# Moving one of ten chunks a tile from VectorE to ScalarE, dropping the first layer's split, and reordering the products behind the loop

## What is computed

```python
x = x0
for k in (k0, k1, k2):                       # (128, 40, 40), (128, 128, 40), (128, 128, 40)
    x = jnp.einsum('bhd,bmd,ohm->bod', x, x0, k)
    outputs.append(jnp.sum(x, axis=-1))      # (512, 128) each
z = jnp.concatenate(outputs, axis=1)
h = jnp.concatenate([z, dense_ctx], axis=1)  # 384 + 16 columns
h = jnp.maximum(h @ W_top1 + b_top1, 0.0)    # 512 wide
h = jnp.maximum(h @ W_top2 + b_top2, 0.0)    # 256 wide
y = h @ W_top3
```

## Time and profile before

| | |
|---|---|
| median of three runs | 759.55 us (759.42 to 760.4) |
| profiled execution, its own time | 758.94 us |
| span of the profiled execution | 757.0 us |
| busy: TensorE, VectorE, ScalarE, GpSimd | 663.1, 669.6, 531.2, 279.2 us |

### The profile page before, as it was taken

How to read it: one execution, slowest core, us unless ns; L and a number is a source line. 1 busy time by engine, 2 the same in 40 slices (tenths; PEclk the granted TensorE clock), 3 DMA queues, 4 the chain that set the end, 5 groups by cost and what they waited for, 6 DMA issues and landing times.

```text
span 757.0 us, 12101 instructions
## 1 busy us (share of the span) xinstructions
PE 663.1 (88%) x2558; PEld 471.8 (62%) x2558; DVE 669.6 (88%) x1607; ACT 531.2 (70%) x1753; POOL 279.2 (37%) x250
## 2 busy tenths in 40 slices
PE   0389999898989898999889898989898989997998
PEld 0256666666657676766666676767676666673483
DVE  2579999999899999999899999999999999999291
ACT  1266878786677778786778677777768686786293
POOL 6453444545343536353343535353636311010000
PEclk9999999999999999999999999999999999996699
DMA  6421222121213031211212121213021214100000
GB/s 199 113 77 47 68 48 69 43 73 43 75 29 86 17 87 29 57 45 48 70 43 73 42 74 29 86 29 87 16 71 41 56 49 178 46 1 28 0 1 1
DMA packets 56675, 43.04 MB, mean 57 GB/s; under 512 B 37008, under 2 KB 40336, under 8 KB 56353
## 3 DMA queue, kind: packets, MB, share of 16 engines
q1 hardware_dynamic: 51488, 41.08, 17.8%
q0 software_dynamic: 5120, 1.32, 1.7%
HBM read 40.41 MB, written 1.97 MB: 56 GB/s over the span
## 4 chain that ended last, share of the span: by engine, by line
PE 55%; DVE 27%; issue 10%; ACT 3%; DMA 2%; DVEq 2%; POOL 1%; SPq 1%; ACTq 0%
PE Y L608 11%; PE Y L610 11%; PE Y L609 11%; DVE sums L520 11%; PE X L575 7%; DVE sums L476 5%; DVE sums L481 5%; PE GB L582 3%; DVE pairs_lo L453 3%; ACT sums L401 2%; DVE sums L467 2%; PE X L569 2%; PE X L636 1%; PE X L634 1%; PE X L635 1%
## 5 line engine op out<-in xcount | busy, mean ns | idle before, releaser
L401 ACT ACTIVATE sums<-Y,xtok 128x128 f32<-128x128 f32 x1536 | 423.3, 381 | 116.4 <-PE Y L610 115.7
L608 PE MATMUL Y<-k1lo,x1hi 128*128 128x512 f32 x640 | 298.6, 467 | 23.5 <-DVE sums L520 21.5
L520 DVE SCALAR_TENSOR_TENSOR sums<-Y,xtok,sums 128x128 f32<-128x128 f32 x1024 | 285.4, 341 | 12.8 <-ACT sums L401 8.0
L610 PE MATMUL Y<-k1hi,x1lo 128*128 128x512 f32 x640 | 252.8, 395 | 0.0
L609 PE MATMUL Y<-k1hi,x1hi 128*128 128x512 f32 x640 | 252.4, 394 | 0.0
L336 POOL TENSOR_TENSOR diag<-xtok,mask 128x320 f32<-128x320 f32 x64 | 82.5, 1289 | 345.6 <-PE GB L582 345.4
L307 POOL DMA_INDIRECT x0g<-in_table,rows_now x160 | 192.0, 1200 | 42.2 <-issue 38.4
L608 PEld LDWEIGHTS Y<-k1lo,x1hi 128*128 128x128 f32 x640 | 120.2, 188 | 81.8 <-DVE sums L520 44.5
L609 PEld LDWEIGHTS Y<-k1hi,x1hi 128*128 128x128 f32 x640 | 120.6, 188 | 41.0 <-issue 14.4
L610 PEld LDWEIGHTS Y<-k1hi,x1lo 128*128 128x128 f32 x640 | 120.3, 188 | 29.5
L446 DVE TENSOR_TENSOR pairs<-pairs,A 120x512 f32<-120x512 f32 x112 | 76.2, 680 | 7.0 <-DMA pairs<-scratch 7.0
(11 more groups left out here) (74 smaller groups left out, 365.5 us busy)
## 6 DMA issues: line engine op xcount, KB each, us to landing
pairs<-scratch SPq DMA_DIRECT2D x112, 240.0 KB
A<-scratch SPq DMA_DIRECT2D x16, 240.0 KB
k1raw<-in_k SPq DMA_DIRECT2D x1, 2560.0 KB, 10.7
x0g<-in_table,rows_now POOLq DMA_INDIRECT x160
k2s<-in_k SPq DMA_DIRECT2D x1, 2560.0 KB, 8.8
scratch<-x0g SPq DMA_DIRECT2D x96, 20.0 KB, 1.7
pairs<-in_w SPq DMA_DIRECT2D x3, 256.0 KB, 2.8
w2s<-in_w SPq DMA_DIRECT2D x1, 512.0 KB, 4.0
```

What stands on the lines that cost most here:

```text
L401: ins = nc.scalar.activation(sums[tile % 2][:, k * O:(k + 1) * O], Y[(NCH * tile + c) % YB][:, i * O:(i + 1) * O], ACT.Copy, scale=xtok[sl ...
L520: nc.vector.scalar_tensor_tensor(out=chain[tile % 2][:, i * O:(i + 1) * O], in0=Y[(NCH * tile + c) % YB][:, i * O:(i + 1) * O], scalar=xto ...
L608: nc.tensor.matmul(y, hi[:, tok], k1lo[:, cols], start=True, stop=False)
L610: nc.tensor.matmul(y, lo[:, tok], k1hi[:, cols], start=False, stop=True).then_inc(s_y, 1)
```

## The change

1. `OWNER` goes from ADAADAADAD to AADAADAADA: ScalarE empties seven chunks of a tile (28 instructions), VectorE three (12), at c = 2, 5 and 8. `sums` has seven parts. `early` gets a second step, which adds parts 0 and 1 to parts 2 and 3, and stands behind chunk 8; `merge` is two adds of 512 columns, one of 256 and one of 128, and stands behind chunk 0 of the next tile.
2. The first layer's seven products are all plain fp32: no `ph`, no `pl`, no split of w0.
3. In the tail the four context products come first, then two z0 products, then the last tile's G, then the other two z0 products. The first 8 of the third layer's 40 fields are fp32 products without a split, ahead of z1's products; 32 triples are left. VectorE's splits of k2 are interleaved with those of G.

```diff
-OWNER = "ADAADAADAD"
+OWNER = "AADAADAADA"
-PLACE = (0, 1, 2, 4, 5, 3)
-EARLY_AT = 7
+PLACE = (0, 1, 2, 4, 5, 3, 6)
+EARLY_AT, EARLY = 8, 2
-MERGE_AT = 1
+MERGE_AT = 0
...
-                elif step[:2] == "ph":
...
-                    nc.scalar.activation(pairs_hi[hi][0:PR, :], pairs[buf][0:PR, :], ACT.Copy).then_inc(s_ph, 1)
...
-                elif step[:2] == "pl":
...
-                    nc.vector.tensor_tensor(pairs_lo[buf][0:PR, :], pairs[buf][0:PR, :],
-                                            pairs_hi[hi][0:PR, :].bitcast(f32), ALU.subtract).then_inc(s_pl, 1)
...
+                t = sums[par]
                 dve.wait_ge(s_yA, NA * (T + 1) + 5)
-                nc.vector.tensor_tensor(sums[par][:, BANK:3 * BANK], sums[par][:, BANK:3 * BANK],
-                                        sums[par][:, 4 * BANK:6 * BANK], ALU.add).then_inc(s_early, 1)
+                nc.vector.tensor_tensor(t[:, BANK:3 * BANK], t[:, BANK:3 * BANK], t[:, 4 * BANK:6 * BANK],
+                                        ALU.add).then_inc(s_early, 1)
+                dve.wait_ge(s_yA, NA * (T + 1) + 6)
+                dve.wait_ge(s_chain, STT * (T + 2))
+                dve.wait_ge(s_early, EARLY * (T + 1) + 1)
+                nc.vector.tensor_tensor(t[:, 0:2 * BANK], t[:, 0:2 * BANK], t[:, 2 * BANK:4 * BANK],
+                                        ALU.add).then_inc(s_early, 1)
 
             def merge(T, par):
 
                 t = sums[par]
-                dve.wait_ge(s_chain, STT * (T + 2))
+                dve.wait_ge(s_early, EARLY * (T + 2))
+                nc.vector.tensor_tensor(t[:, 0:BANK], t[:, 0:BANK], t[:, BANK:2 * BANK],
+                                        ALU.add).then_inc(s_merge, 1)
                 dve.wait_ge(s_yA, NA * (T + 2))
-                dve.wait_ge(s_early, T + 2)
-                nc.vector.tensor_tensor(t[:, 0:2 * BANK], t[:, 0:2 * BANK], t[:, 2 * BANK:4 * BANK],
+                dve.wait_ge(s_merge, MERGE * (T + 2) + 1)
+                nc.vector.tensor_tensor(t[:, 0:BANK], t[:, 0:BANK], t[:, 6 * BANK:7 * BANK],
                                         ALU.add).then_inc(s_merge, 1)
...
-                    if c < NS:
...
-                        nc.tensor.matmul(X1[:, :], w0hi[:, w], lo, start=(c == 0), stop=False)
-                        nc.tensor.matmul(X1[:, :], w0hi[:, w], hi, start=False, stop=False)
-                        nc.tensor.matmul(X1[:, :], w0lo[:, w], hi, start=False,
-                                         stop=(c == NC0 - 1)).then_inc(s_l0, 1)
...
+                    pe.wait_ge(s_prod, n + 1)
+                    nc.tensor.matmul(X1[:, :], w0[:, c * O:(c + 1) * O], pairs[buf][0:PR, :],
+                                     start=(c == 0), stop=(c == NC0 - 1)).then_inc(s_l0, 1)
...
+            def first_bank(i):
+
+                c = NCH - YB + i
+                if OWNER[c] == "A":
+                    pe.wait_ge(s_yA, NA * NTILES + rank(c))
+                else:
+                    pe.wait_ge(s_chain, STT * NTILES + MB * rank(c))
 
             pe.wait_ge(s_mlp, 8 * 16)
-            pe.wait_ge(s_chain, STT * (NTILES + 1))
-            pe.wait_ge(s_yA, NA * (NTILES + 1))
             pe.wait_ge(s_x1free, NG)
             for i in range(H1 // P):
-                o = slice(i * P, (i + 1) * P)
-                nc.tensor.matmul(Y[i][:, :], w1s[0][:, o], z0[:, :], start=True, stop=False)
-                nc.tensor.matmul(Y[i][:, :], w1cs[:, o], ctxs[:, :], start=False, stop=False)
+                first_bank(i)
+                nc.tensor.matmul(Y[i][:, :], w1cs[:, i * P:(i + 1) * P], ctxs[:, :], start=True, stop=False)
+            for i in range(H1 // P):
+                if i == H1 // P // 2:
+                    make_G(NTILES - 1, (NTILES - 1) % 2)
+                nc.tensor.matmul(Y[i][:, :], w1s[0][:, i * P:(i + 1) * P], z0[:, :], start=False, stop=False)
             pe.wait_ge(s_Gout, NTILES + 2)
+            pe.wait_ge(s_k2, 16)
+            for m in range(N4 * MB):
+                nc.tensor.matmul(X1[:, :], k2s[:, m, :], G[:, m, SB:], start=(m == 0), stop=False)
```

More of the change, by code:

```diff
@@ L47 @@
 ROLLS = M + KC * NC0 - 1
-NH = 3
 NR = 4
@@ L57 @@
 PARTS = NA
-PLACE = (0, 1, 2, 4, 5, 3)
-EARLY_AT = 7
+PLACE = (0, 1, 2, 4, 5, 3, 6)
+EARLY_AT, EARLY = 8, 2
 MERGE = 4
-NS = 3
+N4 = 2
 CTX = 16
@@ L82, in position @@
     kind, c = step[:-1], int(step[-1])
-    if kind in ("l0_", "prod"):
-        return int(PROD_AT + PROD_APART * c) + (L0_LAG if kind == "l0_" else 0)
-    return int(PROD_AT + PROD_APART * c) + SPLIT_LAG[kind]
+    return int(PROD_AT + PROD_APART * c) + (L0_LAG if kind == "l0_" else 0)
 def prep_steps():
     names = ["xtok"]
-    for kind, n in (("prod", NC0), ("ph", NS), ("pl", NS), ("l0_", NC0)):
-        names += [f"{kind}{c}" for c in range(n)]
+    for kind in ("prod", "l0_"):
+        names += [f"{kind}{c}" for c in range(NC0)]
     names += X1_LAG
@@ L178, in build @@
         k1raw = over("G", "k1raw", [P, NCH, BANK])
-        w0a, w0b, w0s = (over("G", f"w0{n}", [PR, NC0 * O], skip=4 * (NCH * BANK + i * NC0 * O))
-                         for i, n in enumerate(("a", "b", "s")))
+        w0a, w0b = (over("G", f"w0{n}", [PR, NC0 * O], skip=4 * (NCH * BANK + i * NC0 * O))
+                    for i, n in enumerate(("a", "b")))
         w1s = pairs
@@ L187, in build @@
         k2hi, k2lo = k1hi, k1lo
-        Ghi = x1hi + pairs_hi[0:2]
-        Glo = x1lo + [pairs_hi[2], over("sums1", "Glo3", [P, B], f32r)]
+        Ghi = x1hi + [over("sums1", f"Ghi{i}", [P, B], f32r, skip=4 * B * (i - 2)) for i in (2, 3)]
+        Glo = x1lo + [over("sums1", f"Glo{i}", [P, B], f32r, skip=4 * B * i) for i in (2, 3)]
         h2, ys = G[:, 0:2, 0:B], G[0:1, 2, 0:B]
@@ L356, in prep @@
                         "p (j m k) -> p j m k", m=M, k=KC)[:, :, :, 0], ACT.Copy).then_inc(s_xtok, 1)
-                elif step[:2] == "ph":
-                    c = int(step[2:])
-                    _, hi, free = split(u, slot, c)
-                    n, buf, _ = chunk(u, slot, c)
-                    act.wait_ge(s_prod, n + 1)
-                    if free is not None:
-                        act.wait_ge(s_l0, free)
-                    nc.scalar.activation(pairs_hi[hi][0:PR, :], pairs[buf][0:PR, :], ACT.Copy).then_inc(s_ph, 1)
                 elif step == "x1hi":
```

95 lines of the change are left out of this document (33 added, 62 removed).

## The result

The changed kernel took 727.61 us (median of four runs, 723.17 to 727.84) against 759.48 before; the ratio is 0.9564, 95% interval 0.9527 to 0.9602. The forecast was 703, range 693 to 724. The profiled execution took 727.84 with a span of 725.9; 700.8 had been forecast for the span, so 25.1 us are to be found.

The account below looks back on a forecast made before the run. VectorE was taken to pace at 39.1 us a group, TensorE after the change at 36.6. 757.0 - 40.0 (loop) - 0.4 (last group) - 14.3 (tail) - 1.5 (start) = 700.8 span; with overheads 703 us, range 693 to 724.

Parts of the forecast that it names:

- What bounds the kernel: Loop before the change: VectorE paces with 39.1 us of work a group of 40.57, against TensorE's 36.1 and ScalarE's 30.3.
- the term for VectorE's adds: Loop, per tile: two adds of 1024 columns at 1.14 and 1.25 us, as before; VectorE's tile 7.60, group 35.9.
- GpSimd ... keep their order: Whole kernel: GpSimd, SyncE's queue and the scratch transfers keep their order; no time was put on it.
- The walk of the banks: Clean tile: VectorE's six adds delay TensorE's chunk 7, cycle 8.44 us against 8.54; first-layer work covers the block in other tiles.
- The 0.4 that I added for VectorE's wait for x1hi: Loop: half of the earlier x1hi wait stays, 0.4 us a group, taking 37.5 to 37.9.
- the block holds TensorE also in first-layer tiles: Rival, loop: halfway to the bound, 38.9 us a group and 718 us; chance 0.21.
- The first layer and TensorE's load: Loop: three triples of 0.70 us become fp32 products of 0.86, +0.5 a group; TensorE's load becomes 36.6.
- The share that I gave to the redistribution: Loop: VectorE loses four chain instructions, 1.04 us, and gains an add of 0.70, so 0.34 less a tile.
- ScalarE as the pace: Rival, loop: slower than before through the merge's wait for chunk 9; at 0.36 us a piece, 795 us; chance 0.03.
- The tail: After the loop: TensorE's 55.5 us shrink to 41.2 if the clock stays up, 14.3 us less.
- a fall of the clock: Rival, tail: the context's rest and z0's products run on the low clock, +4 us, 707 us; chance 0.24.
- Ahead of the loop: Before the loop: between 0 and 3 us gained, 1.5 taken, with one fp32 product slower on the low clock.

Follow-up runs that it names:

- e1: Changed kernel with GpSimd's multiplication for diag writing one of 40 fields, most of the third layer left out; 710.45 us.
- e3: Changed kernel with the old chunk distribution, early and merge (ScalarE six chunks, VectorE four), keeping the new first layer and tail; 714.0 us.
- e5: e1 with MERGE_AT = 2, the merge's four adds behind chunk 2's products instead of ahead of them; 685.91 us.
- e9: e3 with G_AT = 8, make_G ahead of the wait for chunk 9's bank; 701.83 us.
- e2: Changed kernel with G_AT = 6 in place of 9, so G and the start of diag come behind chunk 6; 707.45 us.
- e10: Changed kernel with MERGE_AT = 2 alone, the merge behind chunk 2's products, whole diag; 688.93 us.
- e13: Changed kernel with MERGE_AT = 2 and G_AT = 8, tail order unchanged; 687.76 us, ratio 0.9048.
- e7: Changed kernel with GpSimd doing its multiplication for diag twice, the first time into a spare buffer; 757.93 us.
- e6: e2 with z0's four products first in the tail, then two of the context's, G, and the other two; 706.75 us.
- e11: Changed kernel with MERGE_AT = 2, G_AT = 8 and z0's products ahead of the context's in the tail; 688.46 us.
- e4: Changed kernel with the context's four 16-row products replaced by 128-row products of z0, the context left out; 723.36 us.

## Why the prediction was wrong

**What bounds the kernel: half right.** The bank of VectorE's chunk was one wait of TensorE. The same view of the kernel before, 44 to 640 us, has a longer one, which I left out: TensorE waits for VectorE's split of the first layer's products.

```profile
PEld X L569 <- DVE pairs_lo L453: 40.7, 27, 1.9
```

What that was worth shows when a group is taken apart by tiles. The table has the time from the first product of a tile to that of the next on TensorE, the mean of the nine groups among the first twelve that do not stand at a seam of the loop's body (the forecast without its 0.4 for x1hi):

| | tile 0 | tile 1 | tile 2 | tile 3 | sum |
|---|---|---|---|---|---|
| before | 9.22 | 11.99 | 9.98 | 9.27 | 40.46 |
| forecast | 8.44 | 9.62 | 10.13 | 9.27 | 37.46 |
| changed kernel | 9.28 | 9.77 | 10.73 | 9.26 | 39.04 |
| e1, short diag | 8.84 | 9.69 | 10.14 | 9.26 | 37.93 |
| e3, old owners | 9.22 | 9.72 | 10.13 | 9.27 | 38.34 |
| e5, short diag, merge behind 2 | 7.55 | 9.68 | 10.12 | 9.27 | 36.62 |

Dropping the split took 2.3 us out of tile 1 (before against e3), more than the 2.1 that a group gained by it in all. My load of 39.1 for VectorE came near the 40.57 without naming this wait. That the waits named TensorE where ScalarE's first chunk ended last holds too: with G out of that path (e9) the tile fell from 8.54 to 7.99.

**The step that failed is the term for VectorE's adds**, "The two adds of 1024 now follow each other, at 1.14 (677.04 to 678.18) and, dependent, 1.25", with its tile of 7.60 and group of 35.9. In the changed kernel the steps are 1.34 and 1.58 in the clean tile (in the loop 1.25, and 1.68 where an add follows); the next two adds 0.80 and 0.72 where I had 0.70 each. In the sum VectorE's block is 7.24 where the walk had 6.55, and the tile 9.03 where it had 8.44. Two things made it. First, "GpSimd ... keep their order" was true and beside the point: the order between engines moved. The block of adds came to stand where diag starts, and an add waits for diag's 0.75. That is 0.33 a clean tile by these rows, 0.86 a group by e1, so 12.9 us in the loop; in the last group's stretch, 40.1 against 38.8 in e1, 1.3. The plain groups of the table give 1.11; the 0.86 is smaller since e1's own clock was low in its first group. Without this wait the time, e1's 710.45, lies inside the range. The rows of before already held it: diag lasted 1.29 on average and 1.04 in the clean tiles, with an add beside it. I read this as its price, and didn't ask what it is alone. Second, where the next add needs the first the step is 1.25 in the loop and 1.34 in a clean tile, not 1.14: I had taken it from a place where an independent instruction followed. With the next adds this makes 0.36 a clean tile, less 0.08 at its start, which is what e1 and e2 show left, 8.72. Why the steps of a clean tile are longer than those of the loop was not looked into.

**The walk of the banks: right but for its sizes.** It said that the block ahead of chunk 2 holds TensorE by 0.9 in a clean tile and in tile 0, and that TensorE's first-layer work covers it in the other tiles. It is 1.2 in a clean tile. In e1, where diag costs nothing, tiles 1 to 3 are at TensorE's load as forecast (9.69, 10.14, 9.26), and only tile 0 waits, 8.84 against e5's 7.55. So the block is worth 1.3 a group, nearly all in tile 0. The 0.4 that I added for VectorE's wait for x1hi did not come, since that wait is absent from the changed kernel's loop; by luck it stood in for the 0.4 by which tile 0 was too short.

The rival "the block holds TensorE also in first-layer tiles" (0.21, 718) came near with its group of 38.9 and not with its reason. Tile 2 does take 10.73, but in e1 it is back at 10.14: with the wait for diag VectorE's load was about 8.2 x 4 + 5.5 = 38.3, above TensorE's 36.6, and without it, 0.4 a tile less, at 36.7 the two were even, and the block alone does not reach past tile 0. Block and wait together are 39.04 - 36.62 = 2.4 in a plain group; e10 gives most of it back, 39.01 - 36.97 = 2.0, since the collision is smaller there too.

**The first layer and TensorE's load: right.** A product without a split costs 0.86; e5's and e13's groups of 36.75 and 36.80 stand on the load of 36.6. The share that I gave to the redistribution was wrong in sign: it lost some 10 us as made. It gained only with the merge behind chunk 2: e13 is 14 us faster than e9, which has the old distribution, and the loop alone gives 15 x 0.96 = 14.4.

**ScalarE as the pace: excluded, as forecast.** Its piece stayed at 0.265 (19 in 5.03), and VectorE waited for its chunk 9 once in the loop. The rule of the Trainium skill, ScalarE: Activation LUTs, "Rules for kernel authors", that multiplications belong on VectorE, would have spoken against the seven chunks; the measured pieces don't bear it out here.

**The tail: the rival was right here.** The forecast put 0.24 on a fall of the clock and +4; the trace has the fall and +3.8, and by the mean clocks two of the other three runs had it too. With the clock up the sum of 41.2 stands: e7, with the same tail and a clock of 1.00, takes 41.7. TensorE was never idle between 665.4 and 675, and the clock still fell. The rule of the Trainium skill, TensorE: Matmul & The Clock Gate, section "Why this matters for your kernels", that it be kept busy without idle gaps, does not tell this fall. What the rows do have: in all eight traces with a fall in the new tail, in either order, it comes 2.5 to 5.1 us behind the start of the first 16-row product, in e6 and e11 too, where z0's 128-row products had run ahead without one; and e4, without 16-row products, has none in its trace. Against it stand the three traces that have the products and no fall. That their number of rows is the cause was not shown. This stays open.

**Ahead of the loop**: 0.25 gained for 1.5 in the profiled execution. From start to next start the first five products take 1.84, 1.72, 1.45, 0.86 and 0.86 us, so between two and three were slow, not one as I had counted. The windows read a clock of 1.00 there, so that the granted clock does not show why; in the two tails such a product takes 1.7 to 2.0 at the lower level and 0.86 at the higher. Nor is the 0.25 firm: the first x1hi copy comes at 38.3 to 40.2 us in the twelve traces with this first layer, 39.1 on average, and at 40.5 and 41.3 in the two with the old one. By those 1.5 was about right.

## What to carry to other kernels

When work is moved, look at what the other engines do at the new place, and take each duration from a row in which the instruction is alone: an instruction that is longer in some places than in others (here diag, 0.74 to 1.9) is waiting inside its own bar, and what it waits for waits for it in turn. Where a bank or buffer is held by an engine's next instruction, put that instruction ahead of its bookkeeping: the same four adds behind chunk 2 instead of ahead of it were worth 39 us, some 5 of them the clock and the start. Take a group apart by tiles and put each wait of the longest engine into its tile before adding up loads: the wait that dropping the split removed, and the one that the block left, each stood in one tile of four. A step of a chain is not the step between independent instructions; take it from a row where the next one needs the result.

## What the runs showed of the hardware that I had not expected

- GpSimd's multiplication of 128 x 320 takes 0.74 to 0.75 us alone and 1.49 to 1.65 when VectorE adds from two SBUF operands beside it; VectorE's add of 1024 columns takes 1.22 alone and 1.54 to 1.65 behind it. VectorE's instructions with one operand in PSUM stayed at 0.340 to 0.344 on average in all these kernels.
- Even diag of one field of 40 takes 1.1 us on average where it falls into an add (e1), and 0.2 where it does not (most of e5's). GpSimd's price is the rest of the add, whatever its own size. VectorE's price goes by diag's size: the second add takes 1.603 on average behind the whole of diag, 1.234 behind one field, and 1.225 with none beside it (e2).
- TensorE's granted clock fell to half, 1.2 GHz, while it was never idle, behind products of 16 rows (the changed kernel, e11), and traces of the same tail kept it (e2, e5, e7). The tail can so differ by 4 us between executions. It fell inside loops too: at 204 us in the changed kernel, at 202.7 in e4, behind about two microseconds in which TensorE waited. The kernel before had runs of 751.56 and 760.57 with mean clocks of 0.995 and 0.984.
